# Attention on one core: the heads of a group on two halves of TensorE's rows, the split of the row maxima and a copy on GpSimd, and a first stage with four slots

## The reference

```python
qkv = x @ W_qkv.T + b_qkv                    # x: (4, 1024, 128)
scores = jnp.einsum('bhqd,bhkd->bhqk', Q, K) / np.sqrt(D_HEAD)
attn = jax.nn.softmax(scores + causal, axis=-1)
O = jnp.einsum('bhqk,bhkd->bhqd', attn, V)
```

## Time and profile before

| what | value |
|---|---|
| median of 3 runs | 861.89 us (860.15 to 862.83) |
| profiled execution: its time, its span | 859.2 us, 857.6 us |
| busy share of the span PE / PEld / DVE / ACT / POOL | 86 / 38 / 80 / 66 / 49% |
| first stage | 0 to 61.8 us |
| maxima of group 0, then 20 chunks of group 1 | 61.8 to 98.3 us |
| groups with maxima beside the scores | 98.3 to 513.6 us |
| the last scores, without maxima | 513.6 to 549.8 us |
| third stage | 549.8 to 857.6 us |

### The profile page before, as it was taken

One profiled execution on the slowest core, in us unless ns is written; L12 is line 12 of the kernel. 1 busy time (PEld: TensorE's weight loads), 2 busy tenths in 40 slices (PEclk: granted clock), 3 DMA queues, 4 the chain that ended last, 5 costly groups with the idle time before them and its releaser, 6 DMA issues. The chain is left out here.

```text
span 857.6 us, 17568 instructions
## 1 busy us (share of the span) xinstructions
PE 739.3 (86%) x4345; PEld 323.0 (38%) x4345; DVE 683.2 (80%) x2289; ACT 567.2 (66%) x926; POOL 423.4 (49%) x468
## 2 busy tenths in 40 slices
PE   6758999999999999999999998696788888887755
PEld 4432233333332333233323331243456555554345
DVE  5669999898988898898889881156788888888883
ACT  4440267666766676667666767558889797897881
POOL 8655112221222112211222122267899999999984
PEclk9875699999999999999999999987999999999997
DMA  6757535335533653364336331201001101100000
GB/s 174 226 152 198 114 71 132 76 93 116 128 76 84 125 120 75 81 137 116 86 74 137 82 68 33 90 2 52 1 0 38 38 1 37 38 1 13 1 14 25
DMA packets 58955, 67.06 MB, mean 78 GB/s; under 512 B 15488, under 2 KB 33536, under 8 KB 58880
## 3 DMA queue, kind: packets, MB, share of 16 engines
q1 hardware_dynamic: 53120, 62.35, 30.5%
q10 hardware_dynamic: 5184, 2.36, 1.0%
q0 software_dynamic: 576, 1.57, 0.7%
HBM read 46.73 MB, written 19.53 MB: 77 GB/s over the span
## 5 line engine op out<-in xcount | busy, mean ns | idle before, releaser
L697 ACT ACTIVATE probs<-ps 128x384 f32<-128x384 f32 (+2 forms) x384 | 291.9, 810 | 174.4 <-PE ps L751 123.4
L668 POOL TENSOR_SCALAR_AFFINE_SELECT probs<-probs 128x256 f32<-128x256 f32 x256 | 102.9, 407 | 368.6 <-ACT probs L697 366.3
L807 DVE CUSTOM_DVE_ANT_0 junk<-ps,tri 128x256 bf16<-128x256 f32 (+3 forms) x512 | 229.1, 488 | 43.7 <-PE ps L719 36.0
L719 PE MATMUL ps<-Kx,Qx 128*128 128x512 bf16 (+3 forms) x768 | 230.8, 345 | 11.3 <-DVE mx L811 4.1
L751 PE MATMUL ps<-Qa,Ka 128*128 128x512 bf16 (+3 forms) x768 | 185.9, 328 | 15.0 <-DMA Qa<-m_scr 10.1
L737 PE MATMUL ps<-probs,Vg 128*9 128x512 f32 (+3 forms) x1536 | 159.3, 488 | 1.0 <-ACT Os L682 0.5
L811 DVE TENSOR_REDUCE mx<-ps 128x1 f32<-128x512 f32 x256 | 158.2, 679 | 0.3 <-DVE Vg L794 0.2
L719 PEld LDWEIGHTS ps<-Kx,Qx 128*128 128x128 bf16 x768 | 68.7, 97 | 204.4 <-DVE mx L807 124.8
L966 POOL TENSOR_TENSOR S<-sim 128x1024 f32<-128x1024 f32 x64 | 120.6, 1907 | 12.1 <-DVE A L1218 6.5
L1218 DVE SCALAR_TENSOR_TENSOR A<-S,T,ps 128x511 f32<-128x511 f32 x128 | 90.2, 741 | 11.3 <-ACT ps L1040 10.3
L751 PEld LDWEIGHTS ps<-Qa,Ka 128*128 128x128 bf16 x768 | 61.5, 97 | 90.8 <-ACT probs L697 44.3
(11 more groups left out here) (115 smaller groups left out, 868.5 us busy)
## 6 DMA issues: line engine op xcount, KB each, us to landing
Qx<-q_scr SPq DMA_DIRECT2D x48, 192.0 KB
Kx<-k_scr SPq DMA_DIRECT2D x48, 192.0 KB
Qa<-q_scr SPq DMA_DIRECT2D x48, 192.0 KB
Ka<-k_scr SPq DMA_DIRECT2D x48, 192.0 KB
o_scr<-Os SPq DMA_DIRECT2D x32, 256.0 KB, 2.1
q_scr<-qs SPq DMA_DIRECT2D x34, 128.0 KB, 3.3
k_scr<-qs SPq DMA_DIRECT2D x18, 128.0 KB, 3.3
xin<-in_L_attn_x_dram ACTq DMA_DIRECT2D x8, 256.0 KB, 3.7
```

What stands on the lines that cost most here:

```text
L668: pool.affine_select(out=diag, in_=diag, compare_op=ALU.is_ge, fill=0.0, base=0, pattern=[[0, 2], [1, P]], channel_multiplier=-1).then_inc ...
L697: act.activation(probs[:, k % 2, hh, 0:width], ps[:, bank:bank + 2, :].rearrange("p a c -> p (a c)")[:, 0:width], ACT.Exp, scale=SM_SCALE) ...
L719: pe.matmul(ps[:, X_BANK + f % X_SLOTS, 0:c1 - c0], Qx[:, u, hh, P * i:P * (i + 1)], Kx[:, u, hh, c0:c1], start=True, stop=True).then_inc( ...
L807: dve.tensor_tensor_reduce(out=junk[:, f % 4, 0:w], in0=src, in1=tri[:, CHUNK - w:CHUNK], scale=1.0, scalar=-BIG, op0=ALU.add, op1=ALU.max ...
```

## The change

Five things change together.

1. **Two halves of PE's rows.** Operands have 64 rows a head: heads 0 and 1 of a group (`pl` 0 and 1 of half `a` = 0) lie on partitions 0 to 63, heads 2 and 3 on 64 to 127. 64 rows hold 8 of the 9 pairs of parts. The ninth pair and the three rows of the maximum lie in new tiles `Ql` and `Kl`. A chunk of the maxima is one matmul on 64 rows; a step of scores is four: halves 0 and 1 of `Qa`/`Ka`, then halves 0 and 1 of `Ql`/`Kl`, adding into the same two banks. A step is now one key tile of two heads; there are still 24, and 24 exponentials. `MAXC` takes the heads in the order 0, 2, 1, 3.
2. **Slots of `probs`:** four of one key tile each (before, two of two key tiles).
3. **The split on POOL.** DVE makes `rowmax` after chunk 47 as before, POOL makes the parts, and DVE transposes them 6 chunks later (`TURN_LATER`). POOL also copies the values of the next group (`Vg`), before DVE's.
4. **SP's order.** The transfers of the row maximum now stand ahead of the load of the next `Qx`/`Kx`; the row maximum takes four stores and two loads. An operand takes more and longer transfers (rows of 4 KB).
5. **First stage:** four slots of `qs`, loops written out, four stores a half-sequence on SP instead of six (the copies of q's parts are made by the load), no zeroing of `Qx`, `Kx`, `Qa`, `Ka`; the q and k biases come in four transfers instead of one.

`GROUP_ORDER` is another, and `COPY_AT` is (14, 5) instead of (12, 4).

```diff
-GROUP_ORDER = "psxxxpxxsxxsxsxpxspxxsxxpxxxspxxssxxsxpxsxxxsxpxxxsxspsxxsxpxxsxsxxsxpxxsxpxsxsxsxsx"
+GROUP_ORDER = "xxpxxsxsxxpxsxsxpxxsxpxxssxpsxxsxpxsxsxxpxxsxxxxsxsxpxxxssxxpxxssxxpxxssxxpxxssxpxss"
...
+        def load_last(eng, u, g, done):
+            for a in range(2):
+                for dst, scr in ((Ql, q_scr), (Kl, k_scr)):
+                    eng.dma_start(dst[ROWS * a + PARTS:ROWS * a + PARTS + DH, u, :, :].rearrange("p j t -> p (j t)"),
+                                  scr[g, a, PARTS - 1].rearrange("n d j t -> (n d) (j t)")).then_inc(done, 16)
...
-                            act.wait_ge(qk_stored[u], STORES * 16 * b + ONE)
+                            if b > 1:
+                                act.wait_ge(qk_stored[n % QS], STORES * 16)
...
                     def group(n, u, ahead):
                         sp.wait_ge(s_ready, SPG * n + ONE)
                         load_parts(sp, Qa[:, 1 - u], Ka[:, 1 - u], bass.ds(n + 1, 1), sop_loaded[1 - u])
-                        store_o(n, 0)
+                        load_last(sp, 1 - u, bass.ds(n + 1, 1), sop_loaded[1 - u])
+                        if not isinstance(n, int) or n > 0:
+                            store_o(n - 1, 1)
+                        m_rows(n + 1, 1 - u, bass.ds(n + 1, 1))
                         if ahead:
                             load_next_max(n + 3, 1 - u)
-                        m_rows(n + 1, 1 - u, bass.ds(n + 1, 1))
-                        store_o(n, 1)
+                        store_o(n, 0)
...
-                        pe.matmul(ps[:, X_BANK + f % X_SLOTS, 0:c1 - c0], Qx[:, u, hh, P * i:P * (i + 1)],
-                                  Kx[:, u, hh, c0:c1], start=True, stop=True).then_inc(mx_ready, 1)
+                        a, pl = divmod(hh, PL)
+                        rows = slice(ROWS * a, ROWS * (a + 1))
+                        pe.matmul(ps[:, X_BANK + f % X_SLOTS, 0:c1 - c0], Qx[rows, u, pl, P * i:P * (i + 1)],
+                                  Kx[rows, u, pl, c0:c1], start=True, stop=True).then_inc(mx_ready, 1)
...
-                        for j, q0, w, off in UNITS[k][1]:
-                            bank = S_BANK + 2 * (e % 2) + off // CHUNK
-                            mm = pe.matmul(ps[:, bank, off % CHUNK:off % CHUNK + w], Ka[:, u, hh, P * j:P * (j + 1)],
-                                           Qa[:, u, hh, q0:q0 + w], start=True, stop=True)
+                        for q, k, first in ((Qa, Ka, True), (Ql, Kl, False)):
+                            for a in range(2):
+                                rows = slice(ROWS * a, ROWS * (a + 1))
+                                mm = pe.matmul(ps[:, S_BANK + 2 * (e % 2) + a, 0:w], k[rows, u, pl, P * j:P * (j + 1)],
+                                               q[rows, u, pl, q0:q0 + w], start=first, stop=not first)
                         mm.then_inc(s_ready, 1)
```

More of the change, by code:

```diff
@@ L24 @@
 PARTS = 3
-SPLIT_ROWS = PARTS * PARTS * DH
-M_ROW = SPLIT_ROWS
+PL = GH // 2
+ROWS = P // 2
+FULL = PARTS * DH
 VW = DH + 1
@@ L39 @@
 FAR = 1.0e38
[L43 to L46, removed]
+KTILES = []
+for _half in range(2):
+    for _j in range(4 * _half + 4):
         _q0 = max(P * _j, CHUNK * _half)
[L48 to L59, removed]
+        KTILES.append((_half, _j, _q0, CHUNK * (_half + 1) - _q0))
+PPG = len(KTILES)
+HALF_PIECES = sum(_half == 0 for _half, _j, _q0, _w in KTILES)
+DIAG_TILES = [t for t, (_half, _j, _q0, _w) in enumerate(KTILES) if _j >= 4 * _half]
+SPG = PPG * PL
+MPG = len(DIAG_TILES) * PL
+PROB_SLOTS = 4
 MAXC = []
@@ L302, in load_parts @@
         def load_parts(eng, qdst, kdst, g, done):
[L304 to L312, removed]
+            for a in range(2):
+                q, k = [dst[ROWS * a:ROWS * (a + 1)].rearrange("p j t -> p (j t)") for dst in (qdst, kdst)]
+                qsrc = q_scr[g, a].rearrange("n s d j t -> (n s d) (j t)")
+                eng.dma_start(q[0:2 * FULL], qsrc.unsqueeze(0).broadcast_to([2, FULL, PL * SEQ])).then_inc(done, 16)
+                eng.dma_start(q[2 * FULL:ROWS], qsrc[0:ROWS - 2 * FULL]).then_inc(done, 16)
+                for s in range(PARTS):
+                    ksrc = k_scr[g, a, s].rearrange("n d j t -> (n d) (j t)")
+                    times = PARTS if s < PARTS - 1 else PARTS - 1
+                    eng.dma_start(k[FULL * s:FULL * s + DH * times], ksrc.unsqueeze(0).broadcast_to(
+                        [times, DH, PL * SEQ])).then_inc(done, 16)
@@ L490, in _ @@
                     turn(0, 0)
-                    with pe.Fori(0, BATCH - 1) as b:
+                    for b in range(BATCH - 1):
                         turn(b, 1)
@@ L556, in _ @@
                     copy_turned(0, 1)
-                    with dve.Fori(0, BATCH - 1) as b:
+                    for b in range(BATCH - 1):
                         for u in range(2):
@@ L674, in _ @@
+                    split_max(0)
+                    with pool.Fori(0, GROUPS // 2 - 1) as i:
+                        for u in range(2):
+                            group(2 * i + u, u, False)
+                    group(GROUPS - 2, 0, False)
+                    group(GROUPS - 1, 1, True)
                 @block.scalar
```

282 lines of the change are left out of this document (152 added, 130 removed).

## The result

| | median of the runs | profiled execution: span | granted clock |
|---|---|---|---|
| before | 862.36 us (860.15 to 862.99, 4 runs) | 857.6 us | 0.940 |
| after | 1007.44 us (1004.64 to 1009.98, 4 runs) | 1005.4 us | 0.854 |

The ratio is 1.1687 (95% interval 1.1649 to 1.1725). A kernel has a faster and a slower state of execution, and this document compares fast executions alone (one of e6's ten was slow). The forecast was 814 us, with 846 as its upper end: wrong in sign, and by 193 us.

The account below looks back on a forecast made before the run. PE was taken to bound by a little, with a boundary stall and DVE close behind. 859.2 + 1.7 (split) - 42.6 (groups) - 6 (first stage) - 1 (tail) = 811.3, plus 2.7 for the median: 814 us, range 796 to 846.

Parts of the forecast that it names:

- operand loads that come late with their longer queue: Example given for another slower outcome, with no time of its own; chance 0.03.
- Halves of the rows: Scores on PE: two matmuls on different row halves run together as one; PE needs 21.8 to 25.6 us a group.
- the serial rival: PE's paired matmuls run one behind the other, scores take 7.68 us more a group; 939 us, chance 0.07.
- the rival on weight loads: The second pair's weights wait for the first on PE, a group takes 26.9 us; 832 us, chance 0.17.
- DVE as the next bound: In the groups, DVE's floor of 24.4 us plus 1.3 of waits makes a group 25.7 instead of 28.64.
- The row maxima: At the group boundary: issues, landing and loads need 6 us, 9.5 us of DVE cover them, so PE's stall goes.
- they still come late: Rival: row maxima late through POOL's chain or slow stores, 1.8 us a group remains; 840 us, chance 0.12.
- the stall that was put at 1.8 us a group: PE standing still before each group's first scores, waiting for the load of the row maxima; 1.76 us.
- The split in front of group 0: Before the first group DVE waits for POOL's chain, 2.6 us instead of 0.89: +1.7 us (0.9 to 3).
- The first stage: Four slots end ACT's waits for stores, less some for extra bias transfers: -6 us (-8 to 0).
- The tail: After the last chunk, with the third stage: four slots let ACT wait less, -1 us (-3 to +3).
- The ends of the sum: All terms' low and high ends taken together, given as 793 and 848 us.

Follow-up runs that it names:

- e6: e1 with the split of the row maxima and the copy of the values back on DVE, ahead of the next chunks; 865.6 us.
- e1: The changed kernel with its operand loads rewritten so that 8 rows are outermost instead of a repeat of 2 or 3; 838.9 us.
- e9: e10 with a ninth, unused row behind each part in the scratch, so that sources are 3 or 2 blocks of 8 rows; 999.1 us.
- e10: e5 with plain operand loads of 24 or 16 consecutive rows, q's parts five to a half in the scratch (two more stores); 820.5 us.
- e11: e10 with the loops of PE and ACT over groups written out too; 821.4 us.
- e12: e10 with q's parts three to a half in the scratch, q's rows of a half in five loads, four stores a half-sequence; 812.1 us.
- e5: e1 with DVE's loop over pairs of groups written out; 829.1 us.
- e4: The kernel before with only SP's order changed: row maximum transfers ahead of the next operand load of the maxima; 864.8 us.
- e8: e4 with DVE's loop over pairs of groups written out; 847.1 us.
- e3: The changed kernel with only q's repeated load cut in two loads of 24 rows, k's repeats left; 844.0 us.
- e2: The kernel before with each load of q's 24 rows cut into loads of 13 and 11 rows; 891.6 us.
- e7: e1 with the four matmuls of a score step issued half by half instead of in turns; 835.8 us.

## Why the prediction was wrong

**The step that failed** is the fourth of the change's five parts, "An operand takes more and longer transfers". The sum held no term for it; the loads stood as hidden, and "operand loads that come late with their longer queue" got 0.03, as an outcome without a mechanism or a price. The prediction even says of the first ones that "the operand loads behind it are not waited for"; PE waited 16.5 us for them in the changed kernel. A price could be had from the diff, one rule and a row. By the rule that is cited above, which no row of the kernel before shows, the order of the source's dimensions puts 200 rows of a group on one engine. The earlier trace rows has 103 GB/s at a share of 0.46, so 14 GB/s for a working engine: 819 KB at that rate are 58 us, over twice the period. The true rate, 21 GB/s, makes it 38.7. The share of 0.46 looks like room, and the prediction says nothing of it; but it is a mean over 16 engines, and a mean says nothing of the fullest.

**What followed from it.** The bound of the period moved from DVE at 25.7 to DMA engine 0 at 38.7: +13 a group, x 14.5 = 188, and 814 + 188 = 1002 against 1007 measured. PE's clock follows and does not lead. After PE's stop of 6.06 us the window 302.4 to 304.2 was granted 0.50, the lower of the two levels, and there its pairs started 0.42 us apart where they start 0.21 apart at the upper one. With spread loads the clock is back by itself (0.925 in e1, and 0.860 in e9 against 0.931 in e10), though what the lower clock adds to the time was not measured apart.

**The other steps.**
- *Halves of the rows* held: this is PE of the changed kernel at full clock.
```profile
310.98 0.38 PE L798 MATMUL ps<-Qa,Ka 64*128 64x512 bf16 x2
311.19 0.38 PE L798 MATMUL ps<-Ql,Kl 64*128 64x512 bf16 x2
```
A pair takes the 0.38 us of one, the next pair starts 0.21 later. Neither the serial rival (939) nor the rival on weight loads (832) came about.
- *DVE as the next bound* held by the period, 25.5 in e10, e11 and e12, and by the waits of e12.
- *The row maxima*: in e12 they come in time, as forecast. But the sum of 6 us for issues, landing and loads was right only because SP was free. With repeated loads (e5) the rival "they still come late" came true at 1.8 us a group, its very price, through SP's issuing and not through POOL or slow stores.
- *A term that was missing*: DVE's jump, 3 us in every second group. It hid in PE's stall for the row maxima, which the prediction took away without asking what else was standing still at that moment. In e1 it costs 9.8 us, in e4 17.7. And the stall that was put at 1.8 us a group is worth less: with the row maxima in time and the loop written out, a group of the kernel before takes 27.64 us, 1.0 less (e8).
- *The split in front of group 0*, +1.7: in e12 rowmax starts at 81.39 and the transpose at 83.39, 2.00 us where the earlier trace rows had 1.11. +0.9, mis-sized by half: POOL's steps start 0.36 us apart there, where the prediction had 0.5 to 0.6.
- *The first stage*, -6: DVE begins the next one at 54.12 us in the changed kernel, where it was 61.80: -7.7, inside the range. That the first operand load would then be late was not seen; PE waits 16.5 us for it in the changed kernel, 11 in e3 and 7.0 in e12, which takes most of the gain back.
- *The tail*, -1: from the last copy to the end 348.3 us in e12 and 352.1 before, -3.8. The copy lies at another place in the group, so a part of this is bookkeeping.
- *The ends of the sum* come to 793 and 850 us, not 848; the range did not rest on the upper one.

The sum for a kernel whose loads are spread, whose loads are cheap to issue and whose DVE has no jump was 814, and e12 measured 812.1. That it comes so near is in part luck. The first scores start 2.6 us earlier than before (95.7 for 98.3), where the sum has 4.3. From there to the start of the last scores it is 46.9 us less (401.5 for 448.4), where the sum has 43.6 with the tail. Behind them it is 2.2 more (313.1 for 310.9), where it has nothing. The mechanism of PE and DVE was right, and its sizes were off by 2 to 3 us each way; the change as it was written was bound elsewhere.

## What to carry to other kernels

For every transfer that a change reshapes, write down the outermost dimension of both sides, deal the rows out to that many engines, and add up the bytes of the fullest engine in a period; the mean share of the DMA engines hides it. Price the issuing queue in the same way: issues times their length, against the period. And before a stall is taken away, ask what else stands still under it (a loop's jump, a late store), since that is what shows next.

## What the runs showed of the hardware

- **A working DMA engine moved 20.7 GB/s with two or three of them at work** (58.15 MB in 2815 us), and 14.4 in e10, where by the rule 12 to 16 share each operand load (60.27 MB at 31.9% of 16 x 822.7 us). The operand loads move rows of 4 KB in both. What the engines share was not measured.
- **The number of small packets tells how many engines the loads use**: e9 has 4096 packets under 512 B fewer than e10, e1 1408 more than the changed kernel, e2 1152 more than before, each just the difference in engines by the rule.
- **A source in blocks costs the issuing queue, repeated or not**: 0.68 us a load for (8, 3 copies, 2048), 0.69 for (8, 3, 2048) without a copy (e1) and 0.71 to 0.73 for the padded (3, 8, 2048) of e9, against 0.32 to 0.36 for 24 or 16 consecutive rows of the same 4 KB (e10).
- **DVE's jump back cost 2.5 to 3.5 us** in a loop over 96 chunks: e7 has 12.7 us in 5 times, e1 16.9. PE's and ACT's were not to be seen (e11).
- **Matmuls on different halves of the rows start, in the profile, out of program order** (e7). The Trainium skill ("TensorE: Matmul & The Clock Gate", The mechanism) has their starts and ends strictly in the order of issue. The rows of e7 disagree for the starts by 0.08 us; of the ends they show nothing, since these are modelled.
